# A Macaron block with routed experts: one row table after the visit tables, one inverse in two halves, three more memsets between the last scatters

## The reference

```python
x = x + 0.5 * ffn(layernorm(x))      # routed experts
x = x + attn(layernorm(x))           # linear attention
x = x + 0.5 * ffn(layernorm(x))      # the same experts again

# ffn: 4 experts, 128 -> 512 -> 128, each token takes one
idx = argmax(softmax(x @ Wg + bg))
h = gelu(x @ W1[e] + b1[e]);  y = h @ W2[e] + b2[e];  out = y of e == idx

# attn: features of width 32
q = elu(x @ Wq.T @ proj) + 1;  k = elu(x @ Wk.T @ proj) + 1;  v = x @ Wv.T
kv = sum over tokens of k outer v;  out = (q @ kv) / (sum(q) + 1e-8)
```

## Time and profile before

| what | us |
|---|---|
| median of 3 runs | 232.48 |
| lowest and highest | 232.38, 233.05 |
| the profiled execution | 232.38 |
| its span | 230.6 |
| TensorE busy | 205.0 |
| GpSimd busy | 158.9 |
| VectorE busy | 158.2 |
| ScalarE busy | 129.0 |

### The profile page before, as it was taken

One profiled execution on the slowest core, in us unless ns is written; L12 is line 12 of the kernel. 1 busy time (PEld: TensorE's weight loads), 2 busy tenths in 40 slices (PEclk: granted clock), 3 DMA queues, 4 the chain that ended last, 5 costly groups with the idle time before them and its releaser, 6 DMA issues.

```text
span 230.6 us, 6363 instructions
## 1 busy us (share of the span) xinstructions
PE 205.0 (89%) x1786; PEld 192.7 (84%) x1786; DVE 158.2 (69%) x633; ACT 129.0 (56%) x410; POOL 158.9 (69%) x222
## 2 busy tenths in 40 slices
PE   7889999985999989998999899999999999999700
PEld 7879999974899987778999797879899999999700
DVE  2799845459888979899978777899967454544300
ACT  0655057655746578436756568724776666766300
POOL 7223888971738786293274978869788888888775
PEclk9999999999999999999999999999999999999955
DMA  4998378782435553357405653435926867561111
GB/s 100 320 372 284 105 250 297 263 296 73 174 115 181 171 182 97 130 187 284 165 13 199 216 192 98 140 111 196 340 90 228 278 214 236 220 218 48 46 57 46
DMA packets 22502, 41.69 MB, mean 181 GB/s; under 512 B 3635, under 2 KB 8643, under 8 KB 22470
## 3 DMA queue, kind: packets, MB, share of 16 engines
q1 hardware_dynamic: 18496, 34.24, 40.5%
q0 software_dynamic: 3072, 6.82, 11.3%
q10 hardware_dynamic: 902, 0.23, 0.4%
HBM read 9.41 MB, written 6.82 MB: 70 GB/s over the span
## 4 chain that ended last, share of the span: by engine, by line
PE 27%; POOL 17%; DVE 13%; issue 11%; DMA 7%; DVEq 1%; POOLq 0%
PE U L963 11%; PE DN L974 11%; DMA G<-rows,src 7%; POOL out_dram L445 6%; POOL rest L419 4%; POOL G L433 3%; POOL RS L404 2%; DVE ST L790 2%; DVE SL L645 2%; POOL G L409 2%; DVE G L723 1%; DVE G L787 1%; PE TR L954 1%; PE S L1006 1%; PE S L1030 1%
## 5 line engine op out<-in xcount | busy, mean ns | idle before, releaser
L1144 ACT ACTIVATE hT<-U,slab 128x128 f32<-128x128 f32 x304 | 86.4, 370 | 50.1 <-PE U L963 49.2
L974 PE MATMUL DN<-W,hT 128*128 (+1 forms) x608 | 81.5, 277 | 1.7 <-DVE G L723 1.4
L963 PE MATMUL U<-hT_in,slab 128*128 (+1 forms) x608 | 81.8, 278 | 0.3
L974 PEld LDWEIGHTS DN<-W,hT 128*128 128x128 f32 x608 | 73.8, 192 | 2.8 <-issue 2.7
L963 PEld LDWEIGHTS U<-hT_in,slab 128*128 128x128 f32 x608 | 73.9, 192 | 1.8 <-issue 1.1
L433 POOL DMA_INDIRECT G<-rows,src x64 | 62.6, 978 | 13.9 <-issue 9.9
L723 DVE SCALAR_TENSOR_TENSOR G<-DN,mask,G 128x128 f32 (+1 forms) x76 | 26.4, 347 | 28.9 <-PE DN L974 25.8
L419 POOL MEMSET rest<- 128x512 f32 (+1 forms) x75 | 34.3, 457 | 8.5 <-DVE G L723 3.4
L445 POOL DMA_INDIRECT out_dram<-G x32 | 31.5, 983 | 9.0 <-issue 6.5
L699 DVE TENSOR_SCALAR xn<-G 128x128 f32<-128x128 f32 x64 | 22.3, 377 | 7.0 <-DMA G<-rows,src 6.9
L1138 ACT ACTIVATE hT_in<-TR 128x128 f32<-128x128 f32 (+1 forms) x44 | 14.5, 330 | 19.2 <-PE TR L954 18.8
(11 more groups left out here) (163 smaller groups left out, 220.2 us busy)
## 6 DMA issues: line engine op xcount, KB each, us to landing
slab<-W SPq DMA_DIRECT2D x76, 322.0 KB, 3.1
rows<-XR SPq DMA_DIRECT2D x4, 576.0 KB, 4.8
rows<-G SPq DMA_DIRECT2D x8, 288.0 KB, 2.1
X<-in_L_attn_x_dram SPq DMA_DIRECT2D x4, 256.0 KB, 6.5
XR<-in_L_attn_x_dram SPq DMA_DIRECT2D x2, 512.0 KB, 9.3
W<-in_L_ffn_W_dram SPq DMA_DIRECT2D x1, 1024.0 KB, 11.9
W<-in_L_ffn_W_dram SPq DMA_DIRECT2D x4, 256.0 KB, 5.8
G<-rows,src POOLq DMA_INDIRECT x64, 3.1
```

What stands on the lines that cost most here:

```text
L963: i = eng.matmul(U[s % 3][:, c * P:(c + 1) * P], slab[s % NSLAB][:, c * P:(c + 1) * P], hT_in[ph % 2][:, bass.ds(v * P - expert_at[s], P)] ...
L974: i = eng.matmul(DN[s % 2][:, 0:D], hT[s % NHT][:, c * P:(c + 1) * P], W2[:, bass.ds(expert_at[s] + c * NE * D, D)], start=(c == 0 and not ...
L1144: i = eng.activation(hT[s % NHT][:, c * P:(c + 1) * P], U[s % 3][:, c * P:(c + 1) * P], ACT.Gelu, bias=slab[s % NSLAB][:, F + c:F + c + 1])
```

## The change

- In the list of the last scatters `PAIRS1` goes from 5 to 10, so that tiles 6, 8 and 10 of element 1 get a wait for the last issue and a memset of 256 columns.
- `visit_ends` becomes the head of `visit_tables`; at the start `visit_tables(0, 0)` now stands before `route_src(0, 0)`. In the later phases the two stood side by side already.
- In phase 0 TensorE's `inverse` for phase 1 is cut in two: its tiles 0 to 7 at the end of visit 8, its tiles 8 to 15 in visit 9, where all sixteen stood. The inverses of phases 2 and 3 stay.

```diff
-            DONE0, PAIRS1 = FIRST1 - 4, 5
+            DONE0, PAIRS1 = FIRST1 - 4, 10
...
-            def visit_ends():
+            def visit_tables(f, b):
                 e_no = exp_no[:, 1:NE, 0]
...
-
-            def visit_tables(f, b):
                 over_v = [P, NE - 1, VW]
...
             route_hots(0)
-            visit_ends()
+            visit_tables(0, 0)
             route_src(0, 0)
-            visit_tables(0, 0)
             visit_masks(0, 0)
...
-                if ph < B + 1 and v == hot_at + 4:
+                if ph in (1, 2) and v == hot_at + 4:
                     inverse(ph + 1, 0, NG)
+                if ph == 0 and v == hot_at + 4:
+                    inverse(ph + 1, 2, 4)
                 if s + UP_LEAD < 2 * B * V:
                     up(s + UP_LEAD)
...
+                if ph == 0 and v == hot_at + 3:
+                    inverse(ph + 1, 0, 2)
```

## The result

The changed kernel takes 235.36 us (234.99 to 236.17, four runs) against 232.43 us for the kernel before beside it: a ratio of 1.0124, 95% interval 1.0074 to 1.0174. It is slower, by about 2.9 us; I had said 1.7. A later measurement with more executions gave 235.02 us against 232.81 us, 1.0089 (1.0057 to 1.0121). A ratio compares only executions within 1.5% of the fastest of the same kernel, so of a kernel in which TensorE's clock falls in many executions it can leave out some of these.

A forecast was written before the change was run, and what follows sets the result against it. The prediction took GpSimd's queue to bound the kernel at the front and the end; tail 0.7, tables 0.7 and split 0.3 us added 1.7 to 232.38, giving 234.1 us, range 233.2 to 235.6 us.

The forecast's parts named there:

- the case I called likeliest: Whole kernel: the forecast, with its split hidden or not, 233.6 to 234.7 us, given 63%.
- the second rival: TensorE's clock drops in the new gap at the split inverse: some +1.4 us on the sum, 235.5 us; 20%.
- Part 1, the tail: GpSimd's last scatters: three added memsets at 0.23 us each, 0.69 us, taken as 0.7; bounds 0.6 and 0.9 us.
- Part 2, the first row table: VectorE's start: visit tables first delay `tab`, `src` and the first gather by 0.68 us; taken as 0.7, bounds 0 and 0.75.
- Part 3, the order: TensorE's split inverse: up(12) 0.76 us late, 0.3 us remaining after a later wait; bounds 0 and 0.76 us.
- two restarts: TensorE at the split: two gaps of 0.2 us, before down(9) and before up(12), counted in up(12)'s delay.
- the 2.6 us at the end: Kernel's end before the change: the clock fell at about 220.2 us, 2.6 us after TensorE's last work.
- The sum: Whole kernel: tail 0.7, tables 0.7 and split 0.3 make 1.7 us, so 234.1 us.
- The absorbed front: Gathers at 44 to 51 us: landing set by the neighbouring store, so the tables' move costs nothing; 233.4 us, 13%.
- The faster case: VectorE's waits for gathers at the front shrink, 2.9 us come back: 231.2 us, 4%.

The follow-up runs named there:

- e9: The whole change as it is, timed again beside the kernel before: 235.02 us against 232.81 us, ratio 1.0089.
- e10: The changed kernel plus ten dummy float32 matmuls in TensorE's idle time ahead of the inverse's first half: 234.14 us against 232.81 us for the kernel before.
- e11: The kernel before with only the three memsets in the tail, a third time: 233.47 us against 232.30 us, ratio 1.005.
- e2: The kernel before with only the visit tables of phase 0 moved ahead of the row table: 248.81 us against 248.98 us, ratio 1.0021.
- e1: The kernel before with only the three memsets in the tail, first time: 249.58 us against 248.98 us, ratio 0.9991.
- e12: The kernel before with only the inverse of phase 1 in two halves, a third time: 234.24 us against 232.30 us, ratio 1.0025.
- e7: The kernel before with the inverse split and ten dummy matmuls ahead of its first half, second time: 248.82 us against 248.56 us, ratio 1.0013.
- e4: The kernel before with the inverse split and ten dummy matmuls ahead of its first half, first time: 249.04 us against 248.98 us, ratio 1.007.
- e5_tail: The kernel before with only the three memsets in the tail, second time: 249.07 us against 248.56 us, ratio 0.9998.
- e6_split: The kernel before with only the inverse of phase 1 in two halves, second time: 250.75 us against 248.56 us, ratio 1.0058.
- e3_split: The kernel before with only the inverse of phase 1 in two halves, first time: 249.47 us against 248.98 us, ratio 0.9967.
- e8_before_fill: The kernel before, inverse whole, with six dummy matmuls in TensorE's idle time between up(11) and down(9): 248.95 us against 248.56 us, ratio 0.9974.

## Why the prediction was right, and where it was off

The direction was right and 235.36 us is within the range of 233.2 to 235.6 us, but the case I called likeliest, 233.6 to 234.7 us, did not come. What came is the second rival, whose 235.5 us is 0.1 off the first measurement and 0.5 off the later one. The step that failed is the weighing of that rival. That its number came so near is in part luck: its sum has 1.0 us for the tables and the order, of which the spans leave some 0.2 us (below), and the measurement with more executions has 2.2 us in place of the 2.9.

**Part 1, the tail: confirmed.** 0.69 us was worked out and 0.73 was found between the traces, and 0.69 to 0.72 in e9, e10 and e11, by a step of 1.48 to 1.49 us. Nothing covered it. The median of e11 is 1.17 us above before, with the trace's 0.7 well inside the interval of its ratio (0.3 to 2.0 us).

**Part 2, the first row table: right at its head, too large at its end.** `tab` started at 21.84 us (I had 21.96) and the first gather at 22.98 (22.9). But the norm of tile 13 came 0.42 us later and not 0.7, since the gather behind it landed 4.3 us after its issue and not 4.9. In e2 all of the 0.62 us was gone there. From issue to norm that took from 4.0 us (e2) to 6.0 us (e9), and e1 and e11, in which nothing ahead of it was moved, had 5.3 and 4.8 us; it is no property of the order. A second thing I had missed: the first gather needs the row store as well as `src`. In e12, with the tables where they were, it is

```profile
23.01 1.19 POOL L433 DMA_INDIRECT G<-rows,src  x1 [3.34 <-DMA rows<-XR]
```

0.8 us later than in the earlier trace rows, with `src` done by 22.10 us. In e7 and e11, with the tables where they were too, it starts at 23.04 and 23.00 us, 0.8 and 0.9 us after the end of `src`, where 0.3 us is the step in before and in e2; their rows name `src`, which was long done. In such an execution the move of the tables has nothing to delay. In the changed kernel's own trace the step is 0.5 us, so that some 0.2 us of its 0.79 us may be the store's. So the term belongs between 0 and 0.7 us, as the bounds had it, and I took the top. What of the 0.42 us at the norm reaches the last phase can't be told apart from what the rest gave back. The move alone was timed only at 249 us (+0.2%, -0.2 to +0.6%); its price at 232 us stays open.

**Part 3, the order: too large.** The 0.3 us was for two restarts and later matmuls. e10 shows none of it at LGX of visit 12, and e4 and e7 have the split, the gap filled and the same 10.95 us from the norm of tile 13 to LGX as the kernel before. The 0 that I gave as lower bound was the answer.

**The clock: the failed step.** I wrote that the eight matmuls break the gap, and its two parts are each shorter than the 2.6 us at the end. The trace has the idle time at 54.27 to 56.69 us, 2.41 us by its row, and the clock fell at 58.2 us, 1.5 us after TensorE had begun again. So the break did not save it. LGX moved from 0.42 to 1.70 us late in the changed kernel, +1.28, and 1.71 us lie between e9 and e10. At the end of the program e10's mean span is 2.0 us below e9's. The 1.4 us of the prediction was a price against a kernel before that never falls; this one does, in most executions, and that the rival did not have at all.

What I ought to have asked first is how near the kernel before stood to the edge. It has in the same stretch two idle times of TensorE, 0.54 us ahead of the transposes at 52.4 us and 1.41 us ahead of down(9). The first depends on the landing of a gather, the second grew to 2.41 us by the split. Over all fourteen traces, those at 249 us among them, with the time from the norm of tile 13 to LGX of visit 12 in the last column:

| trace | inverse | idle ahead of the transposes, us | idle behind up(11), us | clock at half, us | norm to LGX, us |
|---|---|---|---|---|---|
| before | whole | 0.54 | 1.41 | stays | 10.95 |
| e2_tables | whole | none | 1.21 | stays | 10.95 |
| e11_tail | whole | 0.97 | 1.41 | stays | 10.94 |
| e1_tail | whole | 1.05 | 1.42 | 58.5 to 61.9 | 11.59 |
| e5_tail | whole | none | 1.41 | 60.2 to 63.6 | 11.60 |
| changed kernel | halves | none | 2.41 | 58.2 to 61.6 | 12.23 |
| e6_split | halves | none | 2.41 | 56.8 to 60.2 | 12.23 |
| e9_after | halves | 2.57 | 2.41 | 56.2 to 63.1 | 12.62 |
| e12_split | halves | 2.35 | 1.48, at half clock | 54.1 to 64.3 | 13.22 |
| e3_split | halves | none | 2.41 | 56.5 to 63.3 | 13.45 |
| e4_split_fill | halves | none | filled | stays | 10.95 |
| e7_split_fill | halves | 1.82 | filled, 0.18 | stays | 10.95 |
| e10_after_fill | halves | 2.07 | filled, 0.18 | stays | 10.94 |
| e8_before_fill | whole | none | filled | stays | 10.95 |

With the gap open the clock fell in all five traces with the halves and in two of the five with the inverse whole; with it filled in none of four. Where it stays, the last column is 10.94 or 10.95 us whatever the order, so the order is free up to there. A fall costs 0.64 and 0.65 us on that way with the inverse whole and 1.3 to 2.5 us with the halves.

What decides it in a kernel with the inverse whole stays open. A late gather, which I had in mind, is not enough of an answer: e5_tail has no wait ahead of its transposes, TensorE was busy without a break from 40 to 52 us, and its clock fell; e1_tail and e11_tail differ by 0.08 us in the first idle time, and one fell and the other didn't. In e9 and e12 the gap ahead of the transposes was long too, and in e12 the clock had fallen before the split's own gap began, so there the split is not what started it.

**The sum.** Of the 1.61 us between the two profiled executions the tail has 0.77 from the last phase's first gather, and 0.84 us are left of the 1.70 at 65 us. The rest was given back on the way: the delay is 1.5 us from 64 to 97 us, 1.27 at 106 us and 0.69 where VectorE waits for a gather at 140 us. Of before, and of the changed kernel:

```profile
139.65 0.35 DVE L699 TENSOR_SCALAR xn<-G 128x128 f32<-128x128 f32 x1 [1.70 <-DMA G<-rows,src]
```

```profile
140.34 0.35 DVE L697 TENSOR_SCALAR xn<-G 128x128 f32<-128x128 f32 x1 [1.12 <-DMA G<-rows,src]
```

The spans of the executions beside e9 and e10 let me split the difference, as an estimate from means that are each known to 0.2 or 0.3 us. Before without a second fall has 230.3 us, e10 without one 231.2: 0.9 us for all three edits with the clock kept, of which the tail has 0.7. e9 has 233.4 us, 2.2 more, by the clock. All executions of before have 231.1 us, so the clock costs 0.8 us there already. 0.9 + 2.2 - 0.8 makes 2.3 us, and 2.2 lie between the two means. The clock's part of the change is thus some 1.4 us, as much as the rival had, but as the difference of two losses, where the rival had a single one and none in the kernel before. The 2.9 us of the first comparison are within its interval of 1.7 to 4.0 us.

The absorbed front, with 13%, came true in part (0.42 us instead of 0.7, and 0 in e2), hidden in the total by the clock. The faster case did not come: no wait for a gather shrank by more than the front's delay.

## What to carry to other kernels

An instruction moved forward in a queue takes its wait with it: eight matmuls of half a microsecond, placed ahead of work that was ready, made 1.41 us of idle TensorE into 2.41 us and cost more by the clock (some 2 us of span between e9 and e10) than by their order (nothing that a trace shows). Before such a move add up TensorE's idle times near it, ask which of them varies with a transfer, and don't count on a few short matmuls to break them. And look at the mean granted clock of every execution beside its time: here the median hides two kinds of execution, 1.2 to 1.9 us apart, and an edit can move the time by changing how many are of each. Take the mean clock that divides them from traces in which the fall can be seen. Where matmuls are added as a filler, compare the spans as well as the times.

## What the runs showed of the hardware

- By its mean the granted clock fell a second time in 38 of 57 executions of kernels that leave this stretch as it was, so a single profile without such a fall (the earlier trace rows and all of before's trace up to 220 us) says little on the median.
- At the lower clock eight float32 weight loads of 128 x 128 take 1.78 us instead of 0.97. The clock came back after 3.4 us (the changed kernel, e1, e5, e6), 6.8 or 6.9 us (e3, e9) and 10.2 us (e12). It fell with no idle time of TensorE above 1.41 us in the 20 us before (e5_tail, at 60.2 us).
- In the thirteen traces in which the norm of tile 13 waits for its gather, issued at 46.9 to 50.7 us beside SyncE's slab copies and row stores, the norm began 4.0 to 6.0 us after that issue.
- The executions of the four runs with filler matmuls take 1.8 to 3.0 us more than their span, those of all others 1.7 to 1.8 us.
- Two chips ran every kernel at 249 us at one time each and at 232 us later. The time is lost from 175 to 210 us, where ScalarE and VectorE wait for "remote" up to 7.9 us at once (e8). In that condition a cost of 0.7 us in GpSimd's tail could not be seen.
